# A gather group that starts when the one in front has landed, in a recommendation tower on one core

## The chip, the cores and the metric

The kernel runs on one core of one Trainium2 chip. The metric is the device time of one execution in microseconds, without the profiler: 381.35 us, the median of 3 runs (380.23 to 384.43). One further execution was profiled; its span is 496.1 us.

## What is computed

Of 2048 samples each has 128 dense features and 26 ids, one for each of 26 tables with 128 columns. The tables have between 1000 and 125000 rows.

```python
e = jnp.stack([tbl_0[ids[:, 0]], ..., tbl_25[ids[:, 25]]], axis=1)
combined = jnp.concatenate([dense[:, None, :], e], axis=1)     # 27 vectors of 128 a sample
interactions = jnp.einsum('bfd,bgd->bfg', combined, combined)
z = jnp.concatenate([dense, interactions[:, IU0, IU1]], axis=1)   # the 351 pairs above the diagonal
h = jnp.concatenate([z, dense], axis=1)
h = jnp.maximum(h @ W_top1 + b_top1, 0.0)                      # 607 -> 512
h = jnp.maximum(h @ W_top2 + b_top2, 0.0)                      # 512 -> 256
y = h @ W_top3                                                 # 256 -> 1
```

## The kernel before

The samples are cut into 16 tiles of 128, and these into four blocks of four. A sample's 26 table rows come on two ways:

- 16 of them are gathered by GpSimd: one indirect DMA for each of 16 slots and each tile, 128 rows of 512 B at a time, into `rows[:, t % 2, slot, :]` (lines 679 to 684). There are 256 such gathers. They are issued in groups of four (`GROUPS`); the four of a group add to one semaphore, `gathered[t % 2][g]`, and `landed(t, g)` (line 494) names that semaphore and the value at which all four have arrived.
- 10 of them are looked up by TensorE a block (512 samples) at a time: VectorE (line 1031) and for some ScalarE (lines 863 and 870) make one-hot matrices from the ids, TensorE multiplies them with the whole table, split in a high and a low part (line 727). SP loads the tables (line 582), 448 and 52 KB each, and the ids (line 575). The results are copied by ScalarE (lines 878 and 897).

TensorE's order is written out in advance. It starts with the look-ups of block 0, with the transposes of tile 0 in between (`START`), and then runs for each tile t: the dot products of tile t (`dot_tile`, line 821: four fills of a PSUM bank, 128 small matmuls), then `STEPS[t]`: the transposes of tile t + 1 (`turn_group`, line 806, four groups of four), then look-ups of the next block and the layers of the block before last, merged. `turn_group(t, g)` waits for `landed(t, g)` in line 804. The transposed rows are copied to `all_combined` by VectorE (line 1044, even groups) and ScalarE (line 916, odd groups); the dot products are copied out by ScalarE (line 925) and go through DRAM scratch to the layers (lines 757, 766, 771, 783).

GpSimd has two tiles' worth of room in `rows` (`ROW_TILES`). It gathers tiles 0 and 1 without a wait but for the ids (lines 695 to 697). Then for t = 0 to 13 it waits until tile t is transposed and gathers group 0 of tile t + 2; gathers groups 1 and 2, for t from 1 to 12 each behind a wait on TensorE's progress in the look-ups (`half_done`, line 704); waits for the third fill of the dot products of tile t (line 707), and gathers group 3. GpSimd's stream holds nothing else after the constants at its start.

Of the kernel before, what the change touches and what calls it, by code (L numbers as in the profile page):

```python
# [65 lines left out]
ROW_TILES = 2  # L66
# [60 lines left out]
def group_slots(t, g):  # L127

    sizes = GROUPS[t // PER_BLOCK]
    first = sum(sizes[:g])  # L130
    return range(first, first + sizes[g])


def n_groups(t):
    return len(GROUPS[t // PER_BLOCK])


def groups_by(t):

    return sum(n_groups(i) for i in range(t + 1))  # L140
# [22 lines left out]
def gathered_by(t, g):  # L163

    return sum(len(group_slots(i, g)) for i in range(t % ROW_TILES, t + 1, ROW_TILES) if g < n_groups(i))
# [53 lines left out]
def halves_beside(t, g):  # L219

    before = 2 * IN_BLOCK[0] + sum(HALVES_AFTER[i // PER_BLOCK][i % PER_BLOCK] for i in range(t - 1))
    return before + 1 + (g - 1) * HALVES_AFTER[(t - 1) // PER_BLOCK][(t - 1) % PER_BLOCK] // 2
# [140 lines left out]
def build(nc, dense, ids, ids_by_feature, tables, W1, b1, W2, b2, W3, y):  # L363
    with ExitStack() as ctx:
# [129 lines left out]
        def landed(t, g):  # L494

            return gathered[t % ROW_TILES][g], 16 * gathered_by(t, g)
# [180 lines left out]
        @block.gpsimd  # L677
        def _(pool):
            def gather(t, groups):
                for g in groups:  # L680
                    for slot in group_slots(t, g):
                        nc.gpsimd.indirect_dma_start(  # L682
                            rows[:, t % ROW_TILES, slot, :], None, tables[SLOT_FEATURES[slot]][:, :],
                            bass.IndirectOffsetOnAxis(ap=all_ids[:, t, slot:slot + 1], axis=0)).then_inc(gathered[t % ROW_TILES][g], 16)

            nc.gpsimd.memset(ones[:], 1.0).then_inc(ones_ready, 1)
            nc.gpsimd.memset(identity[:], 0.0).then_inc(identity_cleared, 1)
            nc.gpsimd.memset(all_combined[:, P * VECTORS:], 0.0).then_inc(constants_ready, 1)
            for c in chunk_row:
                nc.gpsimd.iota(chunk_row[c][:], pattern=[[1, c]], base=0, channel_multiplier=c,  # L690
                               allow_small_or_imprecise_dtypes=True).then_inc(constants_ready, 1)
            pool.wait_ge(identity_cleared, 1)
            nc.gpsimd.affine_select(out=identity[:], in_=identity[:], compare_op=ALU.not_equal, fill=1.0, base=0,
                                    pattern=[[-1, P]], channel_multiplier=1).then_inc(constants_ready, 1)
            pool.wait_ge(ids_loaded, 16)
            for t in range(ROW_TILES):
                gather(t, range(n_groups(t)))
            for t in range(TILES - ROW_TILES):

                pool.wait_ge(turned_done, groups_by(t))  # L700
                gather(t + ROW_TILES, range(1))
                for g in range(1, n_groups(t + ROW_TILES) - 1):
                    if 0 < t <= LAST * PER_BLOCK:
                        pool.wait_ge(half_done, halves_beside(t, g))
                    gather(t + ROW_TILES, range(g, g + 1))

                pool.wait_ge(dots_done, (t + 1) * FILLS - 1)
                gather(t + ROW_TILES, range(n_groups(t + ROW_TILES) - 1, n_groups(t + ROW_TILES)))
# [448 lines left out]
```

## Time and profile before

| | |
|---|---|
| median of the timed runs | 381.35 us (380.23 to 384.43, 3 runs) |
| span of the profiled execution | 496.1 us |
| GpSimd busy in it | 254.8 us, 266 instructions |
| TensorE busy in it | 376.0 us |
| VectorE busy, ScalarE busy | 244.4 us, 195.0 us |
| gathers | 256, mean 992 ns each |
| mean granted TensorE clock | 0.904 |

Busy times are of the profiled execution, whose span is all that the profile gives as its own time; it is 114.8 us longer than the median of the timed runs. A share in percent is of that span. "Issue" is time in which an engine waited for nothing that the profile shows. PE is TensorE's matmuls, PEld its weight loads, DVE VectorE, ACT ScalarE, POOL GpSimd and SPq SyncE's DMA queue. A gather's instruction counts as busy while its descriptors are made; the landing of its data comes later and is no part of it.

### The profile page before, as it was taken

How to read it: one execution, taken by the hardware profiler on the slowest of the kernel's cores; microseconds unless marked ns; L12 is line 12 of the kernel's file. 1: busy time of each engine (PE TensorE's matmuls, PEld its weight loads, DVE VectorE, ACT ScalarE, POOL GpSimd, SP SyncE). 2: the span in 40 equal slices, each digit the busy share in tenths (PEclk: the TensorE clock that was granted, in tenths of full speed). 3: DMA queues.
4: the chain of work that ended last, by engine and by line, in shares of the span. 5: the costliest groups of instructions: out<-in, count | busy, mean ns of one | idle time of the engine just before them, and what ended most of it. 6: DMA issues, size and time to landing. Idle time of an engine off the chain costs nothing.

```text
span 496.1 us, 8109 instructions
## 1 busy us (share of the span) xinstructions
PE 376.0 (76%) x3360; PEld 301.4 (61%) x3360; DVE 244.4 (49%) x174; ACT 195.0 (39%) x261; POOL 254.8 (51%) x266
## 2 busy tenths in 40 slices
PE   1951777858586665978798796969788696879997
PEld 1630656647474554767586666867676455666787
DVE  4740789674919370765725750956566101112133
ACT  3810986414242521525252532434354334344400
POOL 6774540655737363646666554747466564730000
PEclk9985799989989796989998898989899898789899
DMA  8841763259915153456714533536232621123330
GB/s 210 218 134 41 218 187 85 70 156 275 227 29 161 45 155 103 109 150 153 183 46 128 160 87 104 143 93 193 74 89 63 168 73 27 49 63 100 69 71 5
DMA packets 38479, 58.44 MB, mean 118 GB/s; under 512 B 21665, under 2 KB 22561, under 8 KB 38444
## 3 DMA queue, kind: packets, MB, share of 16 engines
q1 hardware_dynamic: 29304, 40.74, 30.3%
q0 software_dynamic: 8192, 16.79, 13.5%
q8 instruction: 26, 0.43, 0.4%
q10 hardware_dynamic: 948, 0.41, 0.4%
q14 instruction: 9, 0.07, 0.0%
HBM read 47.68 MB, written 10.23 MB: 117 GB/s over the span
## 4 chain that ended last, share of the span: by engine, by line
PE 58%; issue 16%; DVE 11%; another core or an unknown queue 8%; SPq 3%; DMA 2%; ACT 2%; DVEq 0%; ACTq 0%
PE look_bank L727 25%; PE short_bank L821 15%; DVE one_hot L1031 8%; PE out_bank L757 6%; PE out_bank L771 4%; PE short_bank L806 4%; PE out_bank L766 3%; SPq L632 2%; DVE all_combined L1044 1%; DVE low_table L1019 1%; DMA spread_ids<-in_ids_by_feature 1%; PE out_bank L783 1%; SPq L621 1%; DMA last_scratch<-all_dots 1%
## 5 line engine op out<-in xcount | busy, mean ns | idle before, releaser
L682 POOL DMA_INDIRECT rows<-in_tbl,all_ids x256 | 253.9, 992 | 191.9 <-PE short_bank L821 81.9
L1031 DVE TENSOR_TENSOR one_hot<-spread_ids,row_bank 128x2048 fp32r<-128x2048 int32 (+3 forms) x80 | 170.7, 2175 | 27.1 <-PE look_bank L727 10.7
L727 PE MATMUL look_bank<-one_hot,high_table 125*128 125x512 f32 x328 | 140.8, 429 | 20.0 <-issue 16.1
L727 PE MATMUL look_bank<-one_hot,low_table 125*128 125x512 f32 x328 | 132.4, 404 | 0.6 <-issue 0.6
L821 PE MATMUL short_bank<-all_combined 128*59 128x54 f32 x2048 | 88.1, 247 | 53.2 <-issue 51.5
L821 PEld LDWEIGHTS short_bank<-all_combined 128*59 128x59 f32 x2048 | 79.7, 162 | 66.7 <-issue 66.5
L1044 DVE COPY all_combined<-short_bank 128x512 f32<-128x512 f32 x32 | 21.8, 691 | 156.2 <-PE short_bank L806 122.3
L727 PEld LDWEIGHTS look_bank<-one_hot,high_table 125*128 125x128 f32 x328 | 64.5, 197 | 40.5 <-issue 23.6
L727 PEld LDWEIGHTS look_bank<-one_hot,low_table 125*128 125x128 f32 x328 | 64.6, 197 | 16.9 <-issue 4.1
L925 ACT COPY all_dots<-short_bank 128x432 f32<-128x432 f32 x64 | 33.1, 518 | 97.1 <-remote 53.7
L878 ACT COPY looked_up<-look_bank 128x512 f32<-128x512 f32 x40 | 23.4, 586 | 120.8 <-remote 45.3
L806 PE MATMUL short_bank<-identity,rows 128*128 128x128 f32 x256 | 40.0, 290 | 38.7 <-issue 22.5
L806 PEld LDWEIGHTS short_bank<-identity,rows 128*128 128x128 f32 x256 | 28.9, 146 | 47.0 <-issue 27.0
L1019 DVE TENSOR_TENSOR low_table<-whole_table,high_table 125x1024 fp32r<-125x1024 f32 (+1 forms) x28 | 34.8, 1243 | 33.5 <-ACT high_table L852 22.7
L897 ACT COPY all_combined<-looked_up 128x1280 f32<-128x1280 f32 (+2 forms) x20 | 39.7, 1985 | 0.2
L852 ACT CAST high_table<-whole_table 125x1024 fp32r<-125x1024 f32 (+1 forms) x28 | 29.7, 1065 | 7.7 <-DMA whole_table<-in_tbl 7.7
L771 PE MATMUL out_bank<-hidden,w 128*128 128x512 f32 (+2 forms) x96 | 32.4, 470 | 0.0
L938 ACT ACTIVATE hidden<-out_bank,bias 128x512 f32<-128x512 f32 x18 | 15.4, 858 | 33.2 <-PE out_bank L757 18.3
L916 ACT COPY all_combined<-short_bank 128x512 f32<-128x512 f32 x32 | 19.9, 674 | 8.4 <-PE short_bank L806 8.4
L771 PEld LDWEIGHTS out_bank<-hidden,w 128*128 128x128 f32 x96 | 16.8, 199 | 6.3 <-issue 4.3
L1053 DVE TENSOR_SCALAR hidden<-out_bank,bias 128x128 f32<-128x128 f32 (+1 forms) x18 | 7.9, 437 | 22.2 <-PE out_bank L766 17.9
L863 ACT ACTIVATE one_hot<-spread_ids,chunk_row 128x512 fp32r<-128x512 int32 x24 | 15.4, 714 | 0.0
(42 smaller groups left out, 183.5 us busy)
## 6 DMA issues: line engine op xcount, KB each, us to landing
whole_table<-in_tbl SPq DMA_DIRECT2D x26, 448.0 KB
spread_ids<-in_ids_by_feature SPq DMA_DIRECT2D x40, 256.0 KB
block_scratch<-all_dots SPq DMA_DIRECT2D x24, 208.0 KB
rows<-in_tbl,all_ids POOLq DMA_INDIRECT x256
block_scratch<-all_dots SPq DMA_DIRECT2D x24, 104.0 KB
pairs<-block_scratch SPq DMA_DIRECT2D x72, 29.2 KB
whole_table<-in_tbl SPq DMA_DIRECT2D x26, 52.0 KB
whole_table<-in_tbl SPq DMA_DIRECT2D x2, 560.0 KB
```

What stands on the lines that cost most here:

```text
L682: nc.gpsimd.indirect_dma_start(rows[:, t % ROW_TILES, slot, :], None, tables[SLOT_FEATURES[slot]][:, :], bass.IndirectOffsetOnAxis(ap=all_ ...
L727: last = nc.tensor.matmul(look_bank[s % LOOK_BANKS][:], table_parts[part][TABLE_PLACE[s]][0:ROWS_K, c, :], one_hot[0:ROWS_K, (chunks_befor ...
L757: last = nc.tensor.matmul(out, w1_parts[weight][0:rows_k, k, i * P:(i + 1) * P], of_parts[of], start=(k == 0 and weight == of), stop=(k == ...
L771: last = nc.tensor.matmul(out, w2[:, k, o * P:(o + 1) * P], hidden1[:, k, a:b], start=(k == 0), stop=(k == last_k))
L806: last = nc.tensor.transpose(turn_bank(t, g)[:, q * P:(q + 1) * P], rows[:, t % ROW_TILES, slot, :], identity[:])
L821: last = nc.tensor.matmul(fill_bank(t, b)[row:row + LOADED, q * SQUARE:(q + 1) * SQUARE], all_combined[:, at:at + LOADED], all_combined[:, ...
L852: nc.scalar.copy(high_table[i][0:ROWS_K, 0:c, :], whole_table[i][0:ROWS_K, 0:c, :]).then_inc(table_high, 1)
L897: nc.scalar.copy(combined[:, :, 1 + GATHERED[m] + slot:1 + GATHERED[m] + slot + b - a], looked_up[:, place:place + b - a, u * P:(u + 1) * ...
L925: nc.scalar.copy(dots_of(h)[:, :, at:at + PER_BANK], fill_bank(t, b)[:, 0:PER_BANK * SQUARE].rearrange("p (q c) -> p c q", q=PER_BANK)).th ...
L1019: nc.vector.tensor_tensor(low_table[i][0:ROWS_K, 0:c, :], whole_table[i][0:ROWS_K, 0:c, :], high_table[i][0:ROWS_K, 0:c, :], ALU.subtract) ...
L1031: last = nc.vector.tensor_tensor(one_hot[:, place:place + n, :], spread_ids[:, s % ID_PLACES:s % ID_PLACES + 1, :].to_broadcast([P, n, COLS]),
L1044: nc.vector.tensor_copy(to, of).then_inc(even_copied, 1)
```

## The change

Before each group of tiles 2 to 15 GpSimd also waits until the group in front, of the same tile or the last one of the tile before, has landed in full. The waits that stood there before stay.

```diff
         def _(pool):
             def gather(t, groups):
                 for g in groups:
+                    if t >= ROW_TILES:
+                        pool.wait_ge(*landed(*((t, g - 1) if g > 0 else (t - 1, n_groups(t - 1) - 1))))
                     for slot in group_slots(t, g):
                         nc.gpsimd.indirect_dma_start(
                             rows[:, t % ROW_TILES, slot, :], None, tables[SLOT_FEATURES[slot]][:, :],
```

## Rows read from the trace of the kernel before

**Rows 1.** Page, span and busy time: engine, us (share of the span), instructions.
```profile
span 496.1 us, 8109 instructions
...
PE 376.0 (76%) x3360; PEld 301.4 (61%) x3360; DVE 244.4 (49%) x174; ACT 195.0 (39%) x261; POOL 254.8 (51%) x266
```

**Rows 2.** Page, the chain that ended last, shares by engine.
```profile
PE 58%; issue 16%; DVE 11%; another core or an unknown queue 8%; SPq 3%; DMA 2%; ACT 2%; DVEq 0%; ACTq 0%
```

**Rows 3.** Windows over the 16 stretches of dot products, line 821 alone.
```profile
core 0: us, PE busy (x) PEld busy (x), PEclk, DMA share, GB/s
84.80:88.20 3.40, 3.40 (x126) 3.40 (x127) 1.00 0.36 82
...
129.20:141.90 12.70, 6.71 (x127) 5.75 (x128) 0.73 0.53 133
155.30:169.40 14.10, 6.25 (x128) 5.50 (x128) 0.76 0.21 51
182.10:196.40 14.30, 6.92 (x128) 5.95 (x128) 0.64 0.41 111
214.60:223.90 9.30, 5.65 (x127) 5.32 (x128) 0.82 0.36 99
...
466.30:469.70 3.40, 3.40 (x127) 3.40 (x128) 1.00 0.14 22
sum 133.70, PE 84.07 PEld 77.59; mean PE 5.25 PEld 4.85
```

**Rows 4.** Tile `short_bank` on TensorE, then its group by lines, both 33 to 53 us.
```profile
L806 PE MATMUL short_bank<-identity,rows x16: 269/370/473, 33.5 to 52.6; 128*128 128x128 f32 x16
...
L806 PE MATMUL short_bank<-identity,rows 128*128 128x128 f32 x16 | 4.5, 351 | 15.0 <-issue 11.3 <-DVE all_combined L1044 3.7
```

**Rows 5.** Timeline of GpSimd: start, us, line, tiles, [idle before]; gathers of tiles 6 and 7.
```profile
195.91 0.94 POOL L682 DMA_INDIRECT rows<-in_tbl,all_ids  x1 [6.11 <-PE short_bank L821]
197.16 0.94 POOL L682 DMA_INDIRECT rows<-in_tbl,all_ids  x1 [0.31 <-issue]
...
199.66 0.94 POOL L682 DMA_INDIRECT rows<-in_tbl,all_ids  x1 [0.30 <-issue]
202.64 1.24 POOL L682 DMA_INDIRECT rows<-in_tbl,all_ids  x1 [2.04 <-PE short_bank L806]
...
217.09 0.94 POOL L682 DMA_INDIRECT rows<-in_tbl,all_ids  x1 [0.30 <-issue]
223.54 0.94 POOL L682 DMA_INDIRECT rows<-in_tbl,all_ids  x1 [5.50 <-PE short_bank L821]
```

**Rows 6.** Timeline of GpSimd, end of tile 1's gathers, tile 2's first and fourth group.
```profile
42.91 0.94 POOL L682 DMA_INDIRECT rows<-in_tbl,all_ids  x1 [0.30 <-issue]
53.25 0.94 POOL L682 DMA_INDIRECT rows<-in_tbl,all_ids  x1 [9.39 <-PE short_bank L806]
...
87.87 0.94 POOL L682 DMA_INDIRECT rows<-in_tbl,all_ids  x1 [19.02 <-PE short_bank L821]
```

**Rows 7.** Chain of waits, 464 to 496 us: start, us, what.
```profile
464.63 0.85 PE short_bank L806 x4
...
494.00 0.16 DVE y_sb L1050
```

**Rows 8.** DMA in 40 slices, 43.86 to 48.4 us: busy tenths; packets; queues.
```profile
DMA  0000008840000000000000000000000000000000
...
q0 software_dynamic: 32, 0.07, 5.5%
```

**Rows 9.** DMA in 40 slices, 68.85 to 74 us, GB/s and queues.
```profile
GB/s 111 191 175 191 191 207 239 223 382 271 366 334 334 334 350 366 334 286 286 286 318 223 207 255 223 318 239 255 270 255 287 80 143 64 48 64 16 0 0 0
...
q1 hardware_dynamic: 535, 0.96, 51.5%
q0 software_dynamic: 82, 0.16, 9.0%
```

**Rows 10.** DMA in 40 slices, 353.53 to 358.5 us, GB/s.
```profile
GB/s 297 198 264 231 231 231 165 198 132 99 0 33 0 0 0 0 0 0 0 0 0 0 0 0 0 132 0 0 0 0 0 0 0 0 0 0 0 0 0 0
```

**Rows 11.** Who waited for whom: us in total, times, longest.
```profile
POOL rows L682 <- PE short_bank L821: 81.9, 14, 19.0
...
ACT high_table L852 <- DMA whole_table<-in_tbl: 7.7, 2, 5.5
...
DVE one_hot L1031 <- DMA spread_ids<-in_ids_by_feature: 3.9, 1, 3.9
```

## The prediction

> **What bounds the kernel now.** I read the page first, then the windows over the dot products, then GpSimd's timeline, then the DMA packets just behind a group of gathers.
>
> The page [rows 1] gives TensorE 376.0 us busy of 496.1 and GpSimd 254.8 us, which looks like an engine with half its time free. The chain that ended last is PE for 58%, with another 16% called "issue" [rows 2]. The reader should distrust both shares, because the profiled execution is 496.1 us long and the median of the timed runs is 381.35 us: 114.8 us exist only while the profiler watches. Where they are is seen in the windows over line 821 [rows 3]. The 128 dot products of a tile take 3.40 us in tiles 0 and 15, but 12.70, 14.10, 14.30 and 9.30 us in tiles 2 to 5. The 16 stretches sum to 133.7 us against 16 x 3.4 = 54.4, so 79.3 us are excess; the granted clock of these stretches is a mean of 0.64 to 0.82 between its two levels (1.2 and 2.4 GHz), where the clean ones have 1.00. The 16 transposes of tile 0 stretch from 33.5 to 52.6 us: 4.5 us busy and 15.0 idle, 11.3 of them for "issue" [rows 4]. So 90.6 of the 114.8 us are visible as TensorE's instructions coming slowly where there are many short ones; I take them to be absent from the timed runs.
>
> Without them a tile is short. In the profile GpSimd's last group of tile 6 starts at 195.91 and that of tile 7 at 223.54 [rows 5], a period of 27.6 us. In the timed run I work it out from the ends. The third fill of tile 0 releases GpSimd at 87.87 [rows 6]; less the 15.0 us that TensorE idled within the tile's transposes [rows 4], that is about 73 us. The tail from tile 15's last transposes at 464.63 to the end is 31.5 us [rows 7]. Between them lie 381 - 73 - 31 = 277 us for 15 tiles, 18.5 us each.
>
> GpSimd's work does not shrink with it. Its gathers start every 1.25 us (195.91, 197.16; [rows 5]), the same before, in and after the stretches where TensorE crawls: 16 gathers are 20.0 us of every 18.5 us tile. GpSimd's own lower bound for the timed run of before is 73 + 53 groups x 5.0 + about 2 for a landing + 31 = 371 us (53: the last group of tile 2 and four groups each of tiles 3 to 15). TensorE's 381 is 10 us above that. **The kernel is bound by TensorE with GpSimd 10 us behind it**, a margin that the profile hides, since in it GpSimd stands still 6.11 + 2.04 us a tile [rows 5].
>
> **The change, part by part.** It removes nothing and moves nothing. It adds 56 waits, one ahead of each group of tiles 2 to 15, on the semaphore of the group in front. Queued behind each wait are four gathers and the rest of GpSimd's stream; who waits for them is the transposes of the same tile two periods later (line 804), and behind these all of TensorE.
>
> 1. The waits themselves. Each is one more sequencer instruction; the nearest row is the 0.30 us between two gathers [rows 5], which is a ceiling, and nothing is the floor. I take 0.1 us.
>
> 2. The landing. Today the next group starts 0.30 us after the last gather of the one in front ends. Afterwards it starts when that gather has landed. From below: in a quiet stretch, after the gather that ends at 43.86 us, only its 32 packets remain, and the ninth of 40 slices of 4.54 us is the last one that moves anything, so it landed 1.0 us after its end [rows 8]. From above: beside a table load (535 packets of SP's queue in the same 5.15 us) the queues move their last bytes in the 37th of 40 slices, 4.8 us behind it [rows 9]. A middling case is 353.53 to 358.50: bytes until the twelfth slice of 4.97 us, 1.5 us, and then only one instruction packet [rows 10]. Most groups have some SP traffic beside them, few a whole table, so I take 1.7 us including the semaphore, nearest to the middling row, and keep 1.2 and 2.4 as ends of a mean over 52 waits.
>
> 3. The sum for one group: start of the first to end of the fourth gather 199.66 + 0.94 - 195.91 = 4.69 us, landing 1.7, wait 0.1, so 6.5 us instead of 5.0. A tile's four groups take 26.0 us.
>
> 4. What hides it. Some of the waits fall where GpSimd stands still anyway: ahead of group 3 (it waits for the dots) and of group 0 (it waits for the transposes). In the profiled execution that covers nearly everything: the period is 27.6 us, 26.0 fit. **I expect its span almost unchanged, 485 to 515 us.** In the timed run the tile is 18.5 us, no idle time is left, and GpSimd falls 7.5 us behind in each. It starts with a lead: a tile's rows are needed one period after its last group is issued. That lead is exactly the 10 us of the two bounds above, and the second or third tile has used it up. From there TensorE waits at each tile's last transposes.
>
> 5. The sum for the timed run: 73 + 53 x 6.5 + 31 = 448.5 us. The other way round: 52 x 1.5 = 78 us added, less the 10 us of margin, on 381.35 gives 449. I take **448 us**, 17% over the median. Once tile 2's own groups 0 to 2 are paced they still end before 73: 43.9 + 3 x 6.5 + 1.3 = 65 us. The half_done waits (line 704) and dots_done waits (line 707) do not add to it; when GpSimd is last, TensorE has long done that work.
>
> The Trainium skill, Perfetto Trace Analysis, section GPSIMD Engine Instruction, says to time such instructions by start-to-start spacing and not by the reported duration. The trace has both: 1.25 us by spacing, 0.94 us by duration [rows 5]; the page's way is the one used in the sum, the other is the second rival.
>
> The Trainium skill, DMA: Bandwidth & Descriptors, section Anatomy of one DMA, puts a fixed cost of about 2.0 us plus bytes over 436e3 on a DMA from GpSimd. For 64 KB that is an estimate of 2.15 us from the issue, so 5.9 us a group with the first three gathers' 3.75, and 6.0 with the wait; the sum would be 73 + 318 + 31 = 422 us. The quiet row says 0.94 + 1.0 us plus a semaphore, which agrees; the loaded rows are longer, and most groups are not in a quiet stretch.
>
> **The rivals.**
>
> *No change.* GpSimd's idle time takes up the waits in the timed run too. For it: the profile, where 8.15 us a tile are idle. Against it: in the timed run there is no such time if 1.25 us a gather holds. It needs a group of at most (381 - 104)/53 = 5.2 us, thus gathers that start every 0.94 us and a landing of 1.4. Time 381 us.
>
> *A smaller loss.* The 0.30 us between gathers belongs to the profiler like TensorE's slow issue, so four gathers take 3.8 us. Then 3.8 + 1.7 + 0.1 = 5.6 us a group and 73 + 297 + 31 = 401 us. Against it: the gap is 0.30 us whether TensorE's issue is slow or not. Shorter landings alone (1.2 us) give 6.0 and 422 us.
>
> *A larger loss.* Landings near 2.4 us on the mean, if more groups lie beside table loads than I think: 4.7 + 2.4 + 0.1 = 7.2 us a group, 486 us.
>
> *Faster.* With gathers spaced out, SP's table and id loads meet fewer gather packets and land sooner. In the profile ScalarE waits 7.7 us for tables and VectorE 3.9 us for ids [rows 11]; at best that comes off and 370 us are left. It decides only if GpSimd does not become the bound, thus at a group under 5.2 us as above.
>
> **How the numbers follow.** Chances: GpSimd the bound at 430 to 470 us 0.57, a smaller loss of 390 to 430 us 0.25, beyond 470 0.05, no change 0.10, faster 0.03. The range: from 400 (the 0.94 us rival) to 470; beyond it are 0.05 above and about 0.15 below. About 1% is what a measurement of this kernel can tell. Faster by over 1% 0.03, within 1% 0.09, slower 0.88.
>
> **What would show it.** In the changed kernel's profile every gather group of tiles 2 to 15 should stand apart from the one in front by 1.2 us or more; the gaps of 0.30 us at 202.64 to 217.09 inside a tile should remain only within fours, with about 1.8 us between fours; GpSimd's wait on TensorE for the dots (81.9 us) should shrink by about 40 us [rows 11], because landing waits eat it. TensorE should show few or no waits for gathers there, and the span should be near 496. The timed median should be far above 381: the profile and the times disagree in direction. I am wrong if the timed median stays within 1%, which would mean that 1.25 us a gather is the profiler's, or that the tile is not 18.5 us; or if the profiled span grows as much as the timed one, which would mean that landings cost more than 2.5 us.

## The result, and the profile after

The changed kernel takes 525.53 us (median of 4 runs, 523.32 to 529.56) against 382.12 us (4 runs in the same comparison): a ratio of 1.378, 95% interval 1.369 to 1.386. I forecast 448 us in 400 to 470. The direction and the mechanism were right, the size was not: on the 381.35 us that the forecast started from, 144 us were lost, where I had 67.

The page of the changed kernel: span, busy time, the chain that ended last, GpSimd's gathers, and a gather's time from issue to landing.

```profile
span 520.9 us, 8161 instructions
...
PE 365.0 (70%) x3360; PEld 294.8 (57%) x3360; DVE 244.8 (47%) x174; ACT 193.6 (37%) x261; POOL 253.6 (49%) x266
...
POOL 33%; DMA 30%; PE 18%; issue 18%; POOLq 0%; DVE 0%
...
L684 POOL DMA_INDIRECT rows<-in_tbl,all_ids x256 | 252.6, 987 | 233.8 <-DMA rows<-in_tbl,all_ids 121.1
...
rows<-in_tbl,all_ids POOLq DMA_INDIRECT x256, 2.6
```

The chain was 58% PE [rows 2]; now GpSimd and its gathers' landings are 63% of it and PE 18%. GpSimd is no busier than before (253.6 against 254.8 us, [rows 1]): its loss is idle time, 233.8 us before gathers. With 0.30 us at some 200 places inside fours taken off, 174 us are left for the 56 places between fours, about 3 us each. Its busy share (49%) does not show that it is the bound.

Who waits for whom in it (us in total, times, longest):

```profile
PE short_bank L808 <- DMA rows<-in_tbl,all_ids: 131.2, 27, 8.8
...
POOL rows L684 <- DMA rows<-in_tbl,all_ids: 121.1, 43, 5.2
```

The 131.2 us are TensorE at its transposes (L808 is L806 of before), waiting for rows; before, no wait of TensorE's transposes ended on a gather. The following is the price of one landing wait, in the changed kernel's chain from 284 to 296 us (start, us, what):

```profile
283.91 2.50 DMA rows<-in_tbl,all_ids
286.41 0.02 issue
286.43 0.02 POOLq L682
286.45 0.72 issue
287.17 0.94 POOL rows L684
...
290.91 3.86 DMA rows<-in_tbl,all_ids
294.77 0.02 issue
294.80 0.02 POOLq L682
294.81 0.72 issue
295.53 0.94 POOL rows L684
```

The fourth gather of a group starts at 283.91. Its instruction takes 0.94 us, its semaphore is complete 2.50 us after the start, so 1.56 us after the end. The wait instruction (POOLq L682) is through at once, and then 0.72 us pass in which nothing waits for anything that the profile shows, before the next gather starts. The second case is the same with a longer landing, 3.86 us. Over the 55 groups from tile 2 on, worked out from the last increment of each group's semaphore, the landing is 2.19 us after the end of the fourth gather (median 1.61) and the start of the next is 0.84 us after it (median 0.76).

### The profile page after: what moved, and what is told of

It is laid out like the page before. It is cut to its first block, busy times and chain, and to the rows that moved or that the text cites. A ratio compares the mean times of both kernels' runs of the same rounds, so it can differ in the third digit from the quotient of the medians.

```text
span 520.9 us, 8161 instructions
## 1 busy us (share of the span) xinstructions
PE 365.0 (70%) x3360; PEld 294.8 (57%) x3360; DVE 244.8 (47%) x174; ACT 193.6 (37%) x261; POOL 253.6 (49%) x266
## 4 chain that ended last, share of the span: by engine, by line
POOL 33%; DMA 30%; PE 18%; issue 18%; POOLq 0%; DVE 0%
POOL rows L684 33%; DMA rows<-in_tbl,all_ids 30%; PE look_bank L729 9%; PE out_bank L768 3%; PE out_bank L773 2%; PE out_bank L759 1%; PE short_bank L808 1%; PE short_bank L823 1%; DMA all_ids<-in_ids 0%; PE out_bank L785 0%; DVE hidden L1055 0%; POOLq L364 0%; POOLq L682 0%; DVE y_sb L1052 0%
## 5 line engine op out<-in xcount | busy, mean ns | idle before, releaser
L684 POOL DMA_INDIRECT rows<-in_tbl,all_ids x256 | 252.6, 987 | 233.8 <-DMA rows<-in_tbl,all_ids 121.1
L729 PE MATMUL look_bank<-one_hot,high_table 125*128 125x512 f32 x328 | 147.6, 450 | 15.6 <-DVE low_table L1021 11.7
L808 PE MATMUL short_bank<-identity,rows 128*128 128x128 f32 x256 | 46.1, 324 | 131.7 <-DMA rows<-in_tbl,all_ids 131.2
L729 PE MATMUL look_bank<-one_hot,low_table 125*128 125x512 f32 x328 | 137.9, 420 | 0.0
L808 PEld LDWEIGHTS short_bank<-identity,rows 128*128 128x128 f32 x256 | 33.1, 164 | 140.1 <-issue 135.5
L729 PEld LDWEIGHTS look_bank<-one_hot,high_table 125*128 125x128 f32 x328 | 68.9, 210 | 37.4 <-DVE low_table L1021 11.2
L729 PEld LDWEIGHTS look_bank<-one_hot,low_table 125*128 125x128 f32 x328 | 68.3, 208 | 17.5 <-issue 3.4
L823 PEld LDWEIGHTS short_bank<-all_combined 128*59 128x59 f32 x2048 | 57.2, 133 | 11.7 <-issue 10.5
L823 PE MATMUL short_bank<-all_combined 128*59 128x54 f32 x2048 | 59.4, 218 | 4.6 <-ACT all_combined L899 2.9
L918 ACT COPY all_combined<-short_bank 128x512 f32<-128x512 f32 x32 | 21.0, 664 | 106.4 <-PE short_bank L808 106.4
```

The costliest lines, as they stand in the source:

```text
L684: nc.gpsimd.indirect_dma_start(rows[:, t % ROW_TILES, slot, :], None, tables[SLOT_FEATURES[slot]][:, :], bass.IndirectOffsetOnAxis(ap=all_ ...
L729: last = nc.tensor.matmul(look_bank[s % LOOK_BANKS][:], table_parts[part][TABLE_PLACE[s]][0:ROWS_K, c, :], one_hot[0:ROWS_K, (chunks_befor ...
L808: last = nc.tensor.transpose(turn_bank(t, g)[:, q * P:(q + 1) * P], rows[:, t % ROW_TILES, slot, :], identity[:])
L823: last = nc.tensor.matmul(fill_bank(t, b)[row:row + LOADED, q * SQUARE:(q + 1) * SQUARE], all_combined[:, at:at + LOADED], all_combined[:, ...
```

## The experiments

Every ratio is to runs of the kernel before in the same comparison, whose medians were 379.91 to 380.08 us in the experiments and 382.12 us in that of the change.

**A second profile of the kernel before.** 

> The kernel before, unchanged, for a second profile. Theory (GpSimd's chain of issue, landing and wake-up is what the change made the bound, and the 496.1 us of the first profile belong to that one execution): a span near 379 us, all 16 stretches of dot products at 3.5 us as in the changed kernel, gathers still 1.25 us apart, GpSimd idle for 1 us a tile or less. Rival (TensorE's slow issue comes with every profiled execution of this kernel): a span near 496 us and stretches of 9 to 14 us again.

It took 383.29 us, with a span of 381.2. Its page, and the windows over the dot products of tiles 2, 4 and 5, which stand in [rows 3] with 12.70, 14.30 and 9.30 us:

```profile
span 381.2 us, 8109 instructions
...
PE 339.9 (89%) x3360; PEld 278.0 (73%) x3360; DVE 243.6 (64%) x174; ACT 193.2 (51%) x261; POOL 264.5 (69%) x266
...
L682 POOL DMA_INDIRECT rows<-in_tbl,all_ids x256 | 263.5, 1029 | 80.9 <-issue 75.9
```

```profile
96.50:100.00 3.50, 3.45 (x126) 3.45 (x128) 1.00 0.84 186
133.50:137.70 4.20, 3.88 (x127) 3.70 (x128) 1.00 0.42 103
153.70:157.20 3.50, 3.50 (x128) 3.50 (x128) 1.00 0.73 196
```

TensorE's slow issue is gone, at a granted clock of 1.00 in these stretches (2.4 GHz); 3.50 us is the usual length and tile 4 has 4.20. So the slow issue belongs to the one execution that the first profile caught and is no part of the timed runs; what caused it there stays open. The prediction's guess of which time was missing holds. What does not hold is what it made of GpSimd. Its timeline from tile 6 to 7 (start, us, [idle before]), and its last gather:

```profile
155.46 0.94 POOL L682 DMA_INDIRECT rows<-in_tbl,all_ids  x1 [0.30 <-issue]
156.71 1.54 POOL L682 DMA_INDIRECT rows<-in_tbl,all_ids  x1 [0.30 <-issue]
158.55 0.95 POOL L682 DMA_INDIRECT rows<-in_tbl,all_ids  x1 [0.30 <-issue]
...
345.01 0.94 POOL L682 DMA_INDIRECT rows<-in_tbl,all_ids  x1 [0.30 <-issue]
```

156.71 is the first gather of tile 7, in front of which the first profile had 2.04 us of waiting [rows 5]. Here no gather after tile 2 waits: all 80.9 us of idle time but 5.0 are the 0.30 us between gathers. And some gathers take longer than 0.94 us, this one 1.54. From 65.83 to 345.96 us 53 groups are issued, 5.29 us each and not 4.99.

**Is it the wait instruction or what it waits for?** Two kernels keep the 56 wait instructions and change what they wait for.

```diff
-pool.wait_ge(*landed(*((t, g - 1) if g > 0 else (t - 1, n_groups(t - 1) - 1))))
+pool.wait_ge(ids_loaded, 16)                                                        # landed_long_ago
+pool.wait_ge(*landed(*((t, g - 2) if g > 1 else (t - 1, n_groups(t - 1) + g - 2))))  # two_in_front
```

> The same 56 wait instructions, each on the load of the ids, which was met before the first gather. Theory: 380 to 386 us, the gaps between fours 0.30 us where nothing else is waited for. Rival A (price of the instruction): 405 to 420 us with gaps of about 1 us.

> The same 56 wait instructions, each on the group two in front. That group landed on the mean 2.2 us after its last gather, 2.6 us or more before this wait is reached. Theory (what costs is the landing of the group just issued plus the 0.76 us from its semaphore to the next gather's start): the waits are met and the time is that of before, 380 to 387 us. Rival A (each wait instruction on GpSimd costs about 0.7 us whether met or not): 56 x 0.7 = 39 us less the margin of some 10, 405 to 420 us. Rival B (the change is slower because fewer gathers in flight move their data more slowly): same as the theory here, since two groups may be in flight.

The wait for the ids gives 380.54 us, ratio 1.001 (0.997 to 1.005). The wait for the group two in front gives 384.66 us, ratio 1.013 (1.008 to 1.019). Rival A, a price of the instruction itself, is out: met waits are free. The 1.3% of the second kernel fits groups whose landing took longer than the next group's issue, in GpSimd's waits there (us in total, times, longest):

```profile
POOL rows L684 <- DMA rows<-in_tbl,all_ids: 5.5, 13, 1.9
```

Most of these 13 are the usual 0.30 us. The long idle times are ahead of groups 0 and 2 of tile 4, 1.89 and 2.46 us, where the group two in front landed 6.1 and 7.5 us after its last gather's end.

So what costs is the landing of the group just issued and what follows it. A second group in flight is enough to hide nearly all of it.

**How many waits.** The wait ahead of group 0 alone (14), and ahead of groups 0 and 2 (28); the change has 56.

```diff
-                    if t >= ROW_TILES:
+                    if t >= ROW_TILES and g == 0:        # first_group_only
+                    if t >= ROW_TILES and g % 2 == 0:    # every_other_group
```

> The landing wait only ahead of group 0 of each tile, 14 in all. Theory: each costs 3.03 - 0.30 = 2.7 us of GpSimd's time, 38 us, less the margin that GpSimd has before; with a margin of 10 to 20 us that is 398 to 410 us. Rival (GpSimd waits ahead of group 0 for the transposes anyway, 1.4 to 2.0 us in the profile of before, so only the rest counts): 14 x 1.3 = 18 us less the margin, 380 to 390 us.

> The landing wait only ahead of groups 0 and 2 of each tile, 28 in all. Theory (price per wait, no margin, since GpSimd issues without a pause in the kernel before): 28 x 2.7 to 3.2 us on 380, less a little because gathers get shorter, 450 to 468 us, halfway between before and the change. Rival (TensorE's waits add to it where GpSimd falls behind, more than in proportion): over 475 us. Rival (half the waits are hidden behind the transposes): under 440 us.

They take 424.11 us, ratio 1.114 (1.106 to 1.121), and 454.67 us, ratio 1.196 (1.190 to 1.202). The first was a miss: I expected 398 to 410 us and got 44 us more than the 379.95 us of before, since I took off a margin of 10 to 20 us, and there is none; the 2.7 us that I put on a wait was too little for these as well. The 14 waits cost 3.2 us each, the 28 cost 2.7, the 56 cost 2.6. Nothing is hidden behind the transposes, as the gap ahead of group 0 is 0.30 us in the clean profile. The waits add up with no first part that is free; few waits cost even more apiece than many.

**More waits in the same stream.** The changed kernel, and a wait after the second gather of each group for these two.

```diff
                     for slot in group_slots(t, g):
+                        if t >= ROW_TILES and slot == group_slots(t, g)[2]:
+                            pool.wait_ge(landed(t, g)[0], landed(t, g)[1] - 32)
```

> The changed kernel with a second wait in the middle of each group of tiles 2 to 15, until its own first two gathers have landed: 56 more waits, each carried by a gather. Theory: landing 1.6 to 2.2 us, start 0.26 us after it, in place of a gap of 0.30 us: 1.6 to 2.1 us each, 90 to 120 us, 612 to 645 us. Rival (the price is that of few gathers in flight, their data moving more slowly, so shorter bursts land sooner): under 600 us. Rival (0.76 us always): 643 to 672 us.

627.26 us in one run, 102 us more for 56 more waits, 1.8 us each. Its chain from 201 to 210 us shows both kinds of wait in turn:

```profile
200.85 2.53 DMA rows<-in_tbl,all_ids
203.37 0.02 issue
203.40 0.02 POOLq L682
203.41 0.72 issue
204.13 0.94 POOL rows L686
205.08 0.30 issue
205.38 2.98 DMA rows<-in_tbl,all_ids
208.36 0.26 issue
208.62 0.94 POOL rows L686
```

At the edge of a group the wait has an instruction of its own, L682, and 0.72 us follow it. In the middle there is no such instruction: the gather carries the wait, and starts 0.26 us after the landing. The landing does not get shorter with two gathers in flight instead of four (2.53 and 2.98 us from the start of the last). Over the 56 waits in the middle of a group it is 1.93 us after the end on the mean (median 1.59), where the changed kernel with four in flight has 2.19 (median 1.61). That speaks against a price of the data's movement: most of it is a latency, paid once a wait.

**The 0.72 us.** At a group's edge a gather stands behind two waits, the landing's and an older one (transposes, look-ups, dots); one rides on it, the other has an instruction of its own. This kernel drops the two older ones that set the pace alone and guard nothing.

```diff
                 for g in range(1, n_groups(t + ROW_TILES) - 1):
-                    if 0 < t <= LAST * PER_BLOCK:
-                        pool.wait_ge(half_done, halves_beside(t, g))
                     gather(t + ROW_TILES, range(g, g + 1))
-                pool.wait_ge(dots_done, (t + 1) * FILLS - 1)
```

> The changed kernel without GpSimd's two waits for pace (TensorE's progress in the look-ups, the third fill of the dot products); the wait for the transposes, which guards the rows, stays. In the changed kernel a landing wait that stands beside such a wait has an instruction of its own and the next gather starts 0.76 us after the semaphore; where it stood alone (tile 15, groups 1 and 2) it started 0.26 us after it. Theory (a wait of its own puts the gather's start-up behind the landing, one that the gather carries lets it run ahead): 38 waits lose 0.5 us each, 19 us, 503 to 509 us. Rival (0.76 us is the time that a late wake-up of GpSimd always takes, and the two rows of tile 15 are chance): 522 to 528 us. Second rival (the pace waits keep gathers off the table loads): slower than 526.

509.22 us, ratio 1.342 (1.334 to 1.350): 16 us less than the changed kernel, and 0.2 us above the range given. Its chain from 176 to 187 us has an edge of each kind:

```profile
176.88 2.48 DMA rows<-in_tbl,all_ids
179.36 0.02 issue
179.38 0.02 POOLq L682
179.40 0.72 issue
180.12 0.94 POOL rows L684
...
183.87 2.50 DMA rows<-in_tbl,all_ids
186.37 0.26 issue
186.62 0.94 POOL rows L684
```

180.12 is group 0 of a tile, which still has two waits: an instruction L682 and 0.72 us. 186.62 is group 1, whose gather carries its one wait: 0.26 us. So it is throughout: 36 of the 42 edges ahead of groups 1, 2 and 3 have 0.26 us here, where the changed kernel has 0.76 at 32 of its 42. So the 0.50 us between the two go with the wait's own instruction. That the start-up of a gather lies behind such an instruction and runs ahead of a wait that the gather carries explains it; what the engine does in these 0.50 us no trace shows.

**TensorE's work.** The changed kernel and the kernel before, each without the product with the low part of the tables in the look-ups; that part of the sum is left out, half of the look-ups' 656 matmuls.

```diff
-                    for part in (HIGH, LOW):
+                    for part in (HIGH,):
...
-                                                start=(c == 0 and part == HIGH), stop=(c == c_all - 1 and part == LOW))
+                                                start=(c == 0 and part == HIGH), stop=(c == c_all - 1))
```

> The changed kernel with the look-ups' product with the low part of the tables left out, 328 of TensorE's matmuls of 512 columns, some 75 us of its time at 0.23 us each. Theory (GpSimd alone is the bound): 518 to 527 us. Rival (TensorE's work still stands on the path behind every landing): 450 to 490 us.

> The kernel before with the look-ups' product with the low part of the tables left out, some 75 us of TensorE's time. What bounds the kernel before: theory (GpSimd issues its gathers without a pause from 3 to 346 us, TensorE is only level with it): 365 to 380 us. Rival (my prediction's step: TensorE bounds it, GpSimd is 10 us behind): 10 us less, then GpSimd is the bound, 370 us; the two differ in the gaps of GpSimd, which are 0.30 us throughout by the theory. Rival B (TensorE alone): 310 to 330 us.

The changed kernel takes 526.53 us without it, ratio 1.387 to before (1.379 to 1.395), and 525.53 with it, while TensorE's busy time falls from 365.0 to 307.4 us. TensorE's look-ups are off the path. The kernel before takes 378.35 us, ratio 0.994 (0.989 to 0.998), for a busy time of TensorE that falls from 339.9 to 287.0 us: it had not been bound by TensorE. Instead TensorE now waits for rows there, and GpSimd still issues without a pause (waits of the kernel before without the low part, TensorE's and GpSimd's, in an execution of 380.36 us):

```profile
PE short_bank L806 <- DMA rows<-in_tbl,all_ids: 39.7, 12, 7.2
```

```profile
POOL rows L682 <- issue: 76.2, 250, 0.3
```

**GpSimd's work.** The kernel before, with the fourth gather of every group from tile 2 on left out, so that the rows of an earlier tile stand in 4 of 16 slots.

```diff
-    return sum(len(group_slots(i, g)) for i in ...
+    return sum(len(group_slots(i, g)) - (i >= ROW_TILES) for i in ...
...
-                    for slot in group_slots(t, g):
+                    for slot in group_slots(t, g)[:4 if t < ROW_TILES else 3]:
```

> The kernel before with the fourth gather of every group of tiles 2 to 15 left out, 56 of 256 (the rows of an earlier tile stand in their place); 75 us of GpSimd's time at 1.33 us each. Theory (GpSimd and TensorE are level): TensorE becomes the bound at once, 365 to 378 us, and GpSimd stands still some 5 us a tile. Rival (GpSimd alone bounds the kernel before): 305 to 330 us.

372.56 us, ratio 0.982 (0.974 to 0.990). 75 us of gathers are gone and 7 us of the time. GpSimd stands still again, in its waits there:

```profile
POOL rows L682 <- PE short_bank L821: 44.0, 13, 5.5
POOL rows L682 <- PE short_bank L806: 8.4, 6, 3.0
```

Taken together, with the start and the tail in both: the kernel needs 378 us when GpSimd is the bound and 373 us when TensorE with what feeds it is. They are level, within 2%, and GpSimd is the later of the two.

## Why the prediction was right or wrong

*The profile's extra 114.8 us are TensorE's slow issue and are absent from the timed runs.* Right: 3.50 to 4.20 us a stretch in the second profile. I put them down to the profiler; they belong to one execution, since the second profile of the same kernel, taken in the same way, does not have them.

*"The kernel is bound by TensorE with GpSimd 10 us behind it."* Wrong, and this is the first step that failed. A group takes 5.29 us and not 4.99, because 24 of the 212 gathers counted take longer than 1.0 us, up to 2.46. I had read one period of 1.25 us from the trace and taken it for all. Over 53 groups that is 16 us, more than the margin. Two more terms of that bound were off: the start of its first group is 65.83 us and not 73, and from the end of the last gather to the end of the span are 35 us and not 33. What makes some gathers long was not tested. It does not follow SP's transfers: in the second profile 11% are long where under 20 KB of SP's queue pass within 1 us of a gather's start, and 15% where over 300 KB do. The bounds by experiment are 378 us for GpSimd and 373 for TensorE. The sum for the changed kernel does not use the margin; the second way to it, 78 us less the 10 of margin, does, and that both gave 449 was luck.

*The sum 73 + 53 x 6.5 + 31.* This is the step that the missed size comes from: the wait and the landing in the 6.5 us of a group. The form was right: the first paced group that the sum counts starts at 76.39, the last gather of all ends at 487.97, and from its landing, 1.6 us later, to the end of the span are 31.3 us. Groups start every (483.29 - 76.39)/52 = 7.83 us, where I had 6.5. The terms, each over 52 or 53 groups:

- The wait, costed at 0.1 us with the 0.30 us gap as a "ceiling": 0.84 us on the mean. This is the largest part, 38 us. The 0.30 us gap is the distance between two gathers whose start-up runs ahead of them; it is no ceiling for a start after a wait.
- The landing, 1.7 us, "nearest to the middling row": 2.19 on the mean, 25 us. The median is 1.61. The rows I had chosen gave the usual case, and the sum wants the mean, which the few long ones set. These lie beside transfers of SP: the 15 landings with 300 KB or more of SP's queue beside them (from the fourth gather's start to 1.5 us after its end) took 3.27 us on the mean, the 27 with under 50 KB took 1.62.
- The issue of four gathers, 4.69 us: 4.82, 7 us.
- The start 3.4 us later, and 2.4 us that lie around the span (523.3 for the profiled execution, 520.9 its span).

448.5 + 38 + 25 + 7 + 3.4 + 2.4 = 524 us, for 525.53. Against the second profile of before it comes out too: groups start 7.83 us apart instead of 5.30, 131.5 us over 52 of them, and the first one starts 10.6 us later (76.39 against 65.83). Less 2.3 us behind the last gather's start that is 139.8 us, and the spans, 520.9 and 381.2, differ by 139.7.

*The profiled span, 485 to 515 us because TensorE's slow issue would cover the waits.* Wrong: 520.9. The slow issue did not return, so nothing covered them.

*The signs.* The fours stand at least 1.78 us apart, where 1.2 was named. GpSimd's wait for the dots, 81.9 us [rows 11], was to shrink by 40 us and is gone. TensorE was to show few or no waits for gathers: it has 131.2 us of them.

*The rivals.* "No change" and "faster" are out. "A smaller loss" by a gap of 0.30 us that belongs to the profiler is out: the clean profile of a run of 383 us has the same gap at 250 places. "A larger loss" with a landing mean near 2.4 us came nearest and was left at 0.05: it had the landing right and missed the start-up.

*The pages.* The fixed cost of 2.0 us a DMA of the Trainium skill (DMA: Bandwidth & Descriptors, section Anatomy of one DMA) gave 422 us. The quiet landings come near it, 2.50 us from a gather's start to its semaphore against an estimate of 2.15, but the sum by it fails for want of the start-up and of the landings beside SP's transfers. The rule of the Trainium skill to time by start-to-start spacing and not by durations (Perfetto Trace Analysis, section GPSIMD Engine Instruction) was right: most gathers start 1.25 us apart in the second profile too, though the mean with the long ones is 1.32.

## What to carry to other kernels

A wait for one's own DMA before the next is issued costs its whole latency each time, here 2.2 us to the semaphore and 0.8 to the next start against 0.30, on an engine that issues without a pause; ask first whether the engine is that, and take the mean of landings and of gathers, not a typical one. If such a throttle is wanted, wait for the group two in front: that cost 1.3% here and not 38%. And where a profiled span is far from the timed median, take a second profile before any engine's idle time is read as slack.

## What the runs showed of the hardware that was not expected

- A GpSimd gather starts 0.26 us after the semaphore if it carries the wait, and 0.76 us after it if the wait is an instruction of its own ahead of it. Met in time, such an instruction costs nothing measurable (ratio 1.001 with 56 waits more, 52 of which stand in the trace as instructions of their own). Every seventh edge took longer, at the same groups in the changed kernel and the one without the pace waits: 1.52 us instead of 0.76 at 8 edges of the first, and 0.82 instead of 0.26 at 6 edges of the second; what that is was not tested.
- The landing of gathers of 64 KB has a floor of 1.5 us after the instruction's end, with two in flight as with four, and a mean of 2.2 us in the changed kernel: 1.62 with next to nothing of SP's queue beside them, 3.27 beside 300 KB or more.
- Gathers issued without a pause take 1029 ns on the mean in the clean profile of before; spaced out by waits they take 987 (the change) and 981 (two waits a group). The rest of the time is the same 944 ns; the long ones get rarer. By these means the change gave back an estimated 10 us of what the waits cost.
- The mean granted TensorE clock fell with TensorE's idle time: 0.973 in the second profile of before, 0.858 in the changed kernel, 0.784 with two waits a group. No price of it shows: without the low part it is 0.771 in the changed kernel, at 526.53 us against 525.53.

Not tried: a version with 15 gathers a tile and 11 look-ups a block, which the two bounds of 378 and 373 us leave little room for. No kernel here beats the kernel before by more than the part of the work that it leaves out.
